# Softmax sums gathered, and their inverses spread, by transfers on GpSimd's queue

## The reference

```
q, k, v = heads(ln(x) @ Wq + bq), heads(ln(x) @ Wk + bk), heads(ln(x) @ Wv + bv)
attn = q @ k.T / sqrt(16) + rel_bias_h[..., None] + rel_bias_w[..., None, :]
out  = softmax(attn) @ v                 # (4*12, 1024, 16)
x    = x + out @ Wp + bp
x    = x + ffn(layernorm(x))             # 192 -> 768 -> 192, weights and activations rounded
```

## Time and profile before

| what | value |
|---|---|
| median of 3 runs | 905.75 us |
| the profiled execution | 904.3 us, its span 902.5 us |
| TensorE busy over the span | 791.0 us (88%) |
| VectorE busy | 743.8 us (82%) |
| ScalarE busy | 558.8 us |
| GpSimd busy | 423.4 us |
| attention, first to last weighing | 205.1 to 778.2 us |
| granted TensorE clock in attention | 1.00 |

### The profile page before, as it was taken

One profiled execution on the slowest core, in us unless ns is written; L12 is line 12 of the kernel. 1 busy time (PEld: TensorE's weight loads), 2 busy tenths in 40 slices (PEclk: granted clock), 3 DMA queues, 4 the chain that ended last, 5 costly groups with the idle time before them and its releaser, 6 DMA issues. The chain is left out here.

```text
span 902.5 us, 15297 instructions
## 1 busy us (share of the span) xinstructions
PE 791.0 (88%) x5848; PEld 407.7 (45%) x5848; DVE 743.8 (82%) x1493; ACT 558.8 (62%) x609; POOL 423.4 (47%) x263
## 2 busy tenths in 40 slices
PE   5899554479999999999999999999999999678874
PEld 2555454134444444444444444444444442256653
DVE  6998855498989988988998999998888894069995
ACT  1333345027777777777777777777777778447773
POOL 3777794436364454637263735445373324112220
PEclk9999788589999999999999999999999999889986
DMA  7676599999439392948567493939395000433411
GB/s 193 212 226 206 164 300 374 256 194 208 90 88 188 77 200 60 205 85 190 111 147 154 109 191 74 198 68 201 63 206 96 13 12 12 134 105 123 140 36 53
DMA packets 65675, 130.06 MB, mean 144 GB/s; under 512 B 9465, under 2 KB 45306, under 8 KB 57146
## 3 DMA queue, kind: packets, MB, share of 16 engines
q1 hardware_dynamic: 57634, 115.95, 56.2%
q10 hardware_dynamic: 7968, 13.13, 4.2%
HBM read 89.73 MB, written 34.60 MB: 138 GB/s over the span
## 5 line engine op out<-in xcount | busy, mean ns | idle before, releaser
L1065 DVE TENSOR_REDUCE at_piece_neg<-at_r_ps 128x1 f32<-128x512 f32 x768 | 482.8, 682 | 68.1 <-PE at_r_ps L935 64.7
L1028 ACT ACTIVATE at_probs<-at_s_ps 128x1024 f32<-128x1024 f32 x384 | 371.9, 1021 | 130.6 <-PE at_s_ps L956 129.3
L935 PE MATMUL at_r_ps<-op_mix_k,op_mix_q 128*128 128x256 f16 (+1 forms) x1920 | 282.0, 257 | 29.9 <-DMA op_mix_q<-bias_parts 17.8
L935 PEld LDWEIGHTS at_r_ps<-op_mix_k,op_mix_q 128*128 128x128 f16 x1920 | 148.2, 98 | 295.1 <-DVE at_piece_neg L1065 194.1
L850 POOL COPY op_mix_q<-op_mix_q 2x4096 f16<-2x4096 f16 x48 | 172.6, 3596 | 231.0 <-ACT op_mix_q L1033 230.5
L956 PE MATMUL at_s_ps<-op_mix_q,op_mix_k 128*128 128x512 f16 x768 | 227.7, 380 | 1.1 <-ACT at_probs L1028 0.5
L970 PE MATMUL at_o_ps<-at_probs,op_v_u 128*32 128x512 f32 x1536 | 204.2, 604 | 0.0
L218 POOL MEMSET op_mix_q<- 2x10240 f32 x12 | 103.5, 8627 | 0.6
L1033 ACT ACTIVATE op_mix_q<-at_r_ps 2x1024 f16<-2x1024 f16 x48 | 48.5, 1011 | 60.7 <-PE at_r_ps L946 60.7
L956 PEld LDWEIGHTS at_s_ps<-op_mix_q,op_mix_k 128*128 128x128 f16 x768 | 73.4, 98 | 19.6 <-ACT at_probs L1028 10.7
L854 POOL TENSOR_TENSOR at_o_sb<-at_o_sb,at_inv_rows 128x512 f32<-128x512 f32 x24 | 30.7, 1280 | 86.2 <-DVE at_inv_rows L1092 86.2
(11 more groups left out here) (121 smaller groups left out, 674.4 us busy)
## 6 DMA issues: line engine op xcount, KB each, us to landing
op_mix_q<-qk_parts SPq DMA_DIRECT2D x48, 640.0 KB, 10.7
op_mix_q<-bias_parts SPq DMA_DIRECT2D x120, 120.0 KB, 10.3
op_mix_q<-bias_parts SPq DMA_DIRECT2D x72, 128.0 KB, 10.3
bias_parts<-op_mix_q ACTq DMA_DIRECT2D x8, 1024.0 KB, 13.1
qk_parts<-op_mix_q SPq DMA_DIRECT2D x24, 256.0 KB, 2.3
v_rows<-pr_v_st SPq DMA_DIRECT2D x8, 768.0 KB, 4.1
op_mix_k<-qk_parts SPq DMA_DIRECT2D x48, 128.0 KB, 13.1
op_v_u<-v_rows SPq DMA_DIRECT2D x12, 512.0 KB, 14.2
```

Source lines behind the costliest of these rows:

```text
L935: last = pe.matmul(r_bank("piece", at)[:, first % GROUP:first % GROUP + n], mix_q[owner.buf][:, variant, j, qt * P:(qt + 1) * P], mix_k[ow ...
L1028: act.activation(probs[n % PRING][:, 2 * pair:2 * pair + 2, :], s_ps[pair][:, :, :], ACT.Exp).then_inc(exp_done, 1)
L1065: dve.tensor_reduce(piece_neg[half][:, i:i + 1], r_bank("piece", at)[:, :], AX_X, ALU.max, negate=True).then_inc(reduced, 1)
```

## The change

VectorE's two transposes go. GpSimd issues a transfer that gathers the four rows of sums (4 x 512) into `sums` (128 x 16), VectorE takes the reciprocal of these, three steps later than its first transpose stood, and GpSimd issues a second transfer of the inverses to `sum_dram`, waits for it, and a third that reads them back into `inv_rows`, each row 32 times. The orders of GpSimd's and SyncE's lists change too.

```diff
-        SUMS_AT = (O_AT[0] + 1, O_AT[1] + 1)
-        INVERT_AT = (SUMS_AT[0] + 1, SUMS_AT[1] + 1)
+        INVERT_AT = (O_AT[0] + 4, O_AT[1] + 4)
...
+            def move_sums(unit, half):
+                count = unit.u * 2 + half
+                pool.wait_ge(o_out, count + 1)
+                need(pool, inv_done, count)
+                pool.dma_start(sums[:, :], o_sb[half][HD:P:SLOT, :].rearrange("j (a b) -> j a b", b=GROUP // SLOT)).then_inc(sums_in, 16)
+
+            def spread_inverse(unit, half):
+                count = unit.u * 2 + half
+                pool.wait_ge(inv_done, count + 1)
+                need(pool, inv_spread, count * 16)
+                pool.dma_start(sum_dram.rearrange("j (a b) -> (j a) b", b=GROUP // SLOT), inv[:, :]).then_inc(inv_out, 16)
+                pool.wait_ge(inv_out, (count + 1) * 16)
+                need(pool, norm_done, count)
+                pool.dma_start(inv_rows[:, :], sum_dram.unsqueeze(1).to_broadcast([QUAD, SLOT, GROUP])).then_inc(inv_spread, 16)
...
             def emit(unit):
+                if not unit.first:
+                    move_sums(unit.after(-1), 1)
                 spread_max(unit, 1, 0)
-                if not unit.first:
-                    pool.wait_ge(max_spread, unit.u * 4 + 3)
-                    normalise(unit.after(-1), 1)
-                    pool.wait_ge(norm_done, unit.u * 2)
...
                     ops.zero_max(pool, unit.after(2).buf)
+                if not unit.first:
+                    spread_inverse(unit.after(-1), 1)
                 spread_max(unit, 1, 1)
+                if not unit.first:
+                    pool.wait_ge(max_spread, unit.u * 4 + 4)
+                    normalise(unit.after(-1), 1)
+                    pool.wait_ge(norm_done, unit.u * 2)
+                move_sums(unit, 0)
                 if not unit.last:
                     spread_max(unit.after(1), 0, 0)
-                pool.wait_ge(max_spread, unit.u * 4 + (4 if unit.last else 5))
+                spread_inverse(unit, 0)
+                if not unit.last:
+                    spread_max(unit.after(1), 0, 1)
+                pool.wait_ge(max_spread, unit.u * 4 + (4 if unit.last else 6))
                 normalise(unit, 0)
                 if not unit.last:
                     pool.wait_ge(norm_done, unit.u * 2 + 1)
-                    spread_max(unit.after(1), 0, 1)
...
+            move_sums(last, 1)
+            spread_inverse(last, 1)
+            normalise(last, 1)
...
             def emit(unit):          # SyncE
-                if not unit.first:
-                    store(unit.after(-1), 1)
...
-                    load(unit.after(2))
+                    ops.load_qkv(sp, nxt.image, nxt.buf)
+                if not unit.first:
+                    store(unit.after(-1), 1)
+                if nxt.u < UNITS:
+                    ops.load_bias(sp, nxt.u, nxt.buf)
                 store(unit, 0)
...
-            def turn_sums(unit, half):
-
-                dve.wait_ge(o_out, unit.u * 2 + half + 1)
-                dve.transpose(turned[:, :], o_sb[half][:, :]).then_inc(sums_turned, 1)
...
-                dve.wait_ge(sums_turned, count)
-                dve.reciprocal(inv[:, :], blocks[:, :, HD]).then_inc(inv_done, 1)
-                dve.wait_ge(inv_done, count)
-                need(dve, norm_done, count - 1)
-                dve.transpose(inv_rows[:, :].rearrange("p (b c) -> p b c", c=SLOT),
-                              inv[:, :].unsqueeze(2).to_broadcast([P, GROUP // SLOT, SLOT])).then_inc(inv_spread, 1)
+                dve.wait_ge(sums_in, count * 16)
+                need(dve, inv_out, (count - 1) * 16)
+                dve.reciprocal(inv[:, :], sums[:, :]).then_inc(inv_done, 1)
```

More of the change, by code:

```diff
@@ L720, in _, with phase_attention @@
                     last.then_inc(lo_done, 1)
-def phase_attention(nc, ops, ffn_in, out_dram):
+def phase_attention(nc, ops, ffn_in, sum_dram, out_dram):
     STEPS = 2 * KT
@@ L739, in phase_attention @@
         inv = ph.sb("inv", [P, GROUP // SLOT], F32)
-        turned = ph.sb("turned", [P, GROUP], F32)
+        sums = ph.sb("sums", [P, GROUP // SLOT], F32)
         inv_rows = ph.sb("inv_rows", [P, GROUP], F32)
@@ L750, in phase_attention @@
         neg_hi, neg_done = (ph.sem(n) for n in ("neg_hi", "neg_done"))
-        o_out, sums_turned, inv_done, inv_spread, norm_done = (
-            ph.sem(n) for n in ("o_out", "sums_turned", "inv_done", "inv_spread", "norm_done"))
+        o_out, sums_in, inv_done, inv_out, inv_spread, norm_done = (
+            ph.sem(n) for n in ("o_out", "sums_in", "inv_done", "inv_out", "inv_spread", "norm_done"))
         o_stored = [ph.sem(f"o_stored{i}") for i in range(2)]
@@ L850, in spread_max @@
                 pool.tensor_copy(rows[:, 1:, :, :], rows[:, 0:1, :, :].to_broadcast([2, ops.VARIANTS - 1, 2, GROUP])).then_inc(max_spread, 1)
+            def move_sums(unit, half):
[11 more added lines that the diff above has]
+                pool.dma_start(inv_rows[:, :], sum_dram.unsqueeze(1).to_broadcast([QUAD, SLOT, GROUP])).then_inc(inv_spread, 16)
             def normalise(unit, half):
-                pool.wait_ge(inv_spread, unit.u * 2 + half + 1)
+                pool.wait_ge(inv_spread, (unit.u * 2 + half + 1) * 16)
                 pool.tensor_tensor(out=o_sb[half][:, :], in0=o_sb[half][:, :], in1=inv_rows[:, :], op=ALU.mult).then_inc(norm_done, 1)
@@ L880, in emit @@
                     pool.wait_ge(norm_done, unit.u * 2 + 1)
-                    spread_max(unit.after(1), 0, 1)
             each_unit(pool, emit)
-            normalise(Unit(UNITS - 1, BATCH - 1, UNITS - 1), 1)
+            last = Unit(UNITS - 1, BATCH - 1, UNITS - 1)
+            move_sums(last, 1)
+            spread_inverse(last, 1)
+            normalise(last, 1)
         @block.sync
         def _(sp):
-            def load(unit):
-                ops.load_qkv(sp, unit.image, unit.buf)
-                ops.load_bias(sp, unit.u, unit.buf)
             def store(unit, half):
@@ L909, in emit @@
                         sp.wait_ge(stored, 32 * 2)
-                if not (isinstance(unit.u, int) and unit.u + 2 >= UNITS):
+                nxt = unit.after(2)
+                if nxt.u < UNITS:
                     need(sp, pv_done, unit.u * STEPS)
-                    load(unit.after(2))
+                    ops.load_qkv(sp, nxt.image, nxt.buf)
+                if not unit.first:
+                    store(unit.after(-1), 1)
+                if nxt.u < UNITS:
+                    ops.load_bias(sp, nxt.u, nxt.buf)
                 store(unit, 0)
@@ L1077, in join_max @@
                 dve.tensor_tensor(neg_max[half][:, rows, 1], row_neg[half][:, rows], neg_max[half][:, rows, 0], ALU.subtract).then_inc(neg_done, 1)
-            def turn_sums(unit, half):
-                dve.wait_ge(o_out, unit.u * 2 + half + 1)
-                dve.transpose(turned[:, :], o_sb[half][:, :]).then_inc(sums_turned, 1)
             def invert(unit, half):
                 count = unit.u * 2 + half + 1
-                blocks = turned[:, :].rearrange("p (b c) -> p b c", c=SLOT)
-                dve.wait_ge(sums_turned, count)
-                dve.reciprocal(inv[:, :], blocks[:, :, HD]).then_inc(inv_done, 1)
-                dve.wait_ge(inv_done, count)
-                need(dve, norm_done, count - 1)
-                dve.transpose(inv_rows[:, :].rearrange("p (b c) -> p b c", c=SLOT),
-                              inv[:, :].unsqueeze(2).to_broadcast([P, GROUP // SLOT, SLOT])).then_inc(inv_spread, 1)
+                dve.wait_ge(sums_in, count * 16)
+                need(dve, inv_out, (count - 1) * 16)
+                dve.reciprocal(inv[:, :], sums[:, :]).then_inc(inv_done, 1)
             def step_pieces(unit, n):
@@ L1114, in emit @@
                     for half, owner in ((1, None if unit.first else unit.after(-1)), (0, unit)):
-                        if owner and n == SUMS_AT[1 - half]:
-                            turn_sums(owner, half)
                         if owner and n == INVERT_AT[1 - half]:
@@ L1121, in _ @@
             last = Unit(UNITS - 1, BATCH - 1, UNITS - 1)
-            turn_sums(last, 1)
             invert(last, 1)
@@ L1487, in build @@
     att_dram = nc.dram_tensor("att", (GROUPS, P, NQUAD, GROUP), F32).ap()
+    sum_dram = nc.dram_tensor("sum_rows", (QUAD, GROUP), F32).ap()
     with ExitStack() as kept:
@@ L1498, in build @@
                 phase_rel_bias(nc, tables, bias_dram, ops, weights)
-            phase_attention(nc, ops, ffn_in, att_dram)
+            phase_attention(nc, ops, ffn_in, sum_dram, att_dram)
         phase_ffn(nc, ffn_in, weights, out)
```

## The result

The changed kernel takes 944.84 us (median; 940.43 to 950.52) against 905.87 before: ratio 1.043, 95% interval 1.037 to 1.050.

The account below looks back on a forecast made before the run. The prediction took TensorE to pace attention, with VectorE mattering only where it holds TensorE up: 904.3 - 8.1 of stalls + 9.0 at the end = 905.2, with 1.45 for the median 906.6 us. The range was 901 to 917.

Parts of the forecast that it names:

- What bounds the kernel, and what goes: Attention: TensorE sets the pace; of 33.8 us of VectorE's transposes only the stalls count, 8.1 us gained.
- Steps 5 and 13: Attention steps of a unit, one after `invert`, where VectorE's debt stalls TensorE; forecast to fall to 2.84 us.
- the 0.31 us at the unit's seam: TensorE's excess between two units, taken as the order of three banks restarting; forecast to stay.
- The reciprocal in step 5: VectorE's 0.23 us beside a join of maxima; its debt counted at 0, at most 6 us if the cover failed.
- GpSimd's order in half 1: Write landing and read issue before the second copy, due at step 10: 4.45 us against 6.1 free, cost 0.
- rival 2: GpSimd becomes late, holding TensorE at step 10 in units 1 to 9; example 9 us, 915.6 us; chance 0.22.
- The sum: Profiled 904.3 us, less 8.1 of stalls, plus 9.0 at the end: 905.2; with 1.45 for the median, 906.6.
- The end: After the last unit three uncovered transfers make 12.26 us of 3.26: 9.0 us more, bounds +4.6 and +14.2.
- SyncE's order, the gather in the steady state: Attention: q, k, v loads ahead of half 1's store, bias loads behind, cost 0; the gather has 11.6 us to land.
- rival 3: The gather lands too late for VectorE's reciprocal, beyond 11.6 us; at 12.2 it costs 12.6 us, 919; chance 0.07.
- Rivals 1 and 4: rival 1, and that the stalls aren't VectorE's transposes: end costs 9.0, nothing comes back, 914.8 us, chance 0.05.
- rival 1: The transfers are quick, 2.2 us each, so the end costs 5.2 us: 902.9 us; chance 0.28.

Follow-up runs that it names:

- the run with reductions: The changed kernel with VectorE's joins of maxima done by four reductions, the negation too, instead of two-input instructions; 927.26 us (ratio 1.0219).
- the quiet-DMA run: The changed kernel with SyncE waiting until half 1's inverses have landed in DRAM before issuing the q, k, v loads; 1028.3 us (1.1335).

## Why the prediction was wrong, point by point

- *What bounds the kernel, and what goes.* Right. Steps 5 and 13 are plain now, the 0.31 us at the unit's seam is still there, and the gain in attention is 8.0 us against 8.1 forecast. The reciprocal in step 5 costs nothing.
- *GpSimd's order in half 1.* The step that failed, twice. First its size: I put 3.45 us for the landing and 1 for the read's issue, 4.45 against the 6.1 that were free. Measured, 6.3 to 8.5 from write to read and 0.70 for the issue. This was rival 2, in its nine units and at its step, with 1.35 us of lateness a unit where its example had 1.0. I had seen that the write falls among the loads (DMA share 0.94), and still priced it from a median, 3.9 us, that lies between two kinds of store: in the kernel before, nine of the 24 landed in 8.8 to 12.2 us and the other fifteen in 2.0 to 4.1. Measured here, the same write lands in 1.7 us with the DMA idle and in 6.0 to 7.2 with the loads.
- *The same step, its mechanism.* I asked of each moved GpSimd instruction only who waits for its result. Moved by several microseconds, the copy met the join of step 9, and `normalise` that of step 1, and held them though nobody there waits for them. It is no case of mine, and it is the larger part: 15.6 us by the account, 17.6 by the medians of the run with reductions, against 10.4 for the late copies. In the attention of the kernel before no join met a copy. But the hold stood in that trace all the same, in the projections, where I did not look: `pr_rstd`, a tensor_tensor of two SBUF inputs on 4 elements a partition, takes 0.16 us in the two places where GpSimd is idle or clears, and 0.28 to 1.11 us in the six others, each time ending with a tensor_tensor of GpSimd's on other tiles. VectorE twice, then GpSimd (two instructions, the first ends at 75.22):

```profile
7.98 0.16 DVE L483 TENSOR_TENSOR pr_rstd<-pr_rstd 128x4 f32<-128x4 f32 x1 [1.49 <-POOL pr_rstd L448]
```
```profile
74.13 1.11 DVE L483 TENSOR_TENSOR pr_rstd<-pr_rstd 128x4 f32<-128x4 f32 x1 [0.35 <-POOL pr_rstd L448]
```
```profile
74.07 2.27 POOL L457 TENSOR_TENSOR op_mix_q<-op_mix_q 128x512 f16<-128x512 f32 x2
```

  And the Trainium skill states it ("GPSIMD Engine Reference", section 1: SBUF interfaces shared with VectorE, contention with instructions in a 2-port mode or with two SBUF inputs), and the joins are tensor_tensor. By that rule the right question was where in time each copy would come to lie. The runs here agree: 2.48 us instead of 0.17 for two inputs beside a copy, nothing for reductions. They go further on one point, since beside a clearing the same two-input instruction takes its 0.17 us. The tensor_scalar's 3.63 us would fit an instruction in a 2-port mode; that it ran in one no trace shows.
- *TensorE's clock.* The sum has no term for it. Where TensorE stood for a held or late step its granted clock sometimes fell to 0.50: once in this profiled execution (1.6 us), seven times in the run with the last half by VectorE (9.8 us in step 10). The four executions of the changed kernel go from 940.43 us at a mean granted clock of 0.940 to 950.52 at 0.926, so the slower ones probably had more such falls; only the fastest was traced.
- *The end.* With the next phase's loads out of the way the three transfers cost 9.2 us against 9.0 forecast. That is partly luck: landing took 2.2, 2.5 and 5.2 us where I had 3.45 three times, so two terms were too large and the read's too small. I had seen those loads move to about 780 (they went out at 798.90), and asked only whether they would be late themselves, not whom they would meet; they add 4.3 us, within my bounds (+14.2) but not in the value.
- *SyncE's order, the gather in the steady state.* Right as far as it went. The gather took at most 9.7 us to land, under the 11.6 free, so rival 3 did not come; it did in the quiet-DMA run, where VectorE stood 3.3 to 10.5 us before nine reciprocals. Rivals 1 and 4 are out: the transfers of 8 KB are as quick as rival 1 had them only with the DMA idle, the read is nowhere, and the stalls were the transposes'.
- *The sum.* -8.1 + 9.0 became -8.0 + 24.6 + 3.0 + 13.5 + 2.9. The range stopped at 917 because rival 2 was priced at one microsecond a unit and stood alone.

Left open: why the clock falls after some of TensorE's stands and not after others as long, and what the 0.9 us ahead of the first weighing are. The 2.0 us behind the last `normalise` aren't explained either: in the kernel before with only the last half by transfers that stretch is as it was, 120.4 us.

## What to carry to other kernels

Moving work from a busy engine to transfers gains only the stalls that the engine caused (here 8.0 us for 33.8 us of transposes), and costs the landing wherever something else is queued behind it: put what others wait for ahead of the wait, and keep the last round, which nothing covers, on the engine. When a GpSimd instruction moves in time, look at what VectorE runs then, not only at who reads the result; and search the whole trace, not the stage that changes alone, for an instruction that takes several times its usual length. A stall of the engine that sets the pace can cost more than its own length, since its clock may fall behind it: read the granted clock of the stretch before you call the rest unexplained. Price a transfer by the load on the DMA engines at its own moment, and of a load that moves, ask whom it will meet.

## What the runs showed that I had not expected

- VectorE's tensor_tensor with two SBUF inputs stands while GpSimd copies or multiplies (0.17 us becomes up to 3.53), and not while GpSimd clears (0.17); its tensor_scalar from f16 to f32 on SBUF stands while GpSimd clears (3.63 us); tensor_reduce stood in neither case (0.16 to 0.17). The profile counts the time for which an instruction is held as busy.
- The transfers on GpSimd's queue take GpSimd 0.57 to 0.71 us to issue, the very first one 0.91. The DMA view of the changed kernel, issues of that queue (KB each, median us to landing):

```profile
at_inv_rows<-sum_rows POOLq DMA_DIRECT2D x24, 256.0 KB, 5.1
at_sums<-at_o_sb POOLq DMA_DIRECT2D x24, 8.0 KB, 4.9
sum_rows<-at_inv POOLq DMA_DIRECT2D x24, 8.0 KB, 3.6
```

- An 8 KB write lands in 1.7 us with the DMA idle and in up to 7.2 under the loads of the changed kernel; in the quiet-DMA run, under the backed-up bias loads, in 9.6 to 11.6 in eight halves. The broadcast read of 256 KB lands in 4.8 to 5.3 us in all 24 halves of the changed kernel, and in 15.6 to 20.0 when the loads go out with it.
